# A LayerNorm, linear-attention and expert kernel on eight cores: weight conversions queued first, three input buffers, the phi maps in sequence

## The reference

```python
def phi(x): return elu(x) + 1.0
# attention, for every batch row
q = phi(x @ W_q); k = phi(x @ W_k); v = x @ W_v        # H = 64
for t in range(T):                                     # T = 4096, D = 1024
    S = S + outer(k[t], v[t]); z = z + k[t]
    o[t] = (S @ q[t]) / max(sum(z * q[t]), 1e-6)
attn = o @ W_o
# experts
scores = softmax(x @ gate_w.T); top 2 of 16
y = (1, 0, ..., 0)
for e in range(16):
    out = lmlp(x, W1[e], W3[e], W2[e])                 # silu(x W1) * (x W3), W2
    y = where(hit[e], lresnet(y, out, w[e]), y)        # z / sqrt(z0^2 - |z|^2)
ffn = lresnet(y, lmlp(x, Ws1, Ws3, Ws2), 1.0)
# the layer
x = x + layernorm(attn(layernorm(x)))
x = x + layernorm(ffn(layernorm(x)))
```

## Time and profile before

| what | us |
|---|---|
| median of 2 timed runs | 7395.49 (7387.69 to 7403.29) |
| the profiled execution | 7242.95 |
| its span on the slowest core (core 2) | 7241.3 |
| spans of the 8 cores | 7227.3 to 7241.3 |

### The profile page before, as it was taken

How to read it: one execution, slowest core, us unless ns; L and a number is a source line. 1 busy time by engine, 2 the same in 40 slices (tenths; PEclk the granted TensorE clock), 3 DMA queues, 4 the chain that set the end, 5 groups by cost and what they waited for, 6 DMA issues and landing times.

```text
span 7241.3 us, 86010 instructions; the slowest of 8 cores (7227.3 to 7241.3 us)
## 1 busy us (share of the span) xinstructions
PE 4561.7 (63%) x27764; PEld 2806.4 (39%) x27904; DVE 3662.7 (51%) x8672; ACT 3455.1 (48%) x6173; POOL 42.2 (1%) x39
## 2 busy tenths in 40 slices
PE   3112322257778777787776735787777887777671
PEld 2111222244445444454444523455444554445350
DVE  3112444445555555555555344555555555555434
ACT  2111222236655555555555344555656555565434
POOL 0000000000000000000000000000000000000000
PEclk6555555578888888888787867888878888888786
DMA  4998111121111111211111012111111111111102
GB/s 72 120 121 114 44 58 58 58 88 43 57 58 54 46 43 48 65 54 46 43 46 60 21 64 91 65 55 52 43 43 65 55 52 43 43 65 33 57 15 90
DMA packets 355250, 424.53 MB, mean 59 GB/s; under 512 B 46306, under 2 KB 325602, under 8 KB 348658
## 3 DMA queue, kind: packets, MB, share of 16 engines
q1 hardware_dynamic: 349714, 357.44, 15.7%
q0 software_dynamic: 5088, 61.58, 7.5%
HBM read 438.62 MB, written 103.00 MB: 75 GB/s over the span
## 4 chain that ended last, share of the span: by engine, by line
ACT 33%; PE 31%; DVE 17%; issue 9%; another core or an unknown queue 4%; DMA 4%; DVEq 1%; ACTq 1%; SPq 0%; POOL 0%; POOLq 0%
ACT s_sqs L1016 9%; ACT s_sqs L1041 8%; ACT s_y L1074 8%; PE psA L883 5%; PE psB L883 5%; PE psB L894 5%; PE psA L894 5%; PE p_s1C L883 2%; DMA s_x<-x2sp 2%; DVE s_c L335 2%; PE p_gate L737 2%; DVE s_c L1064 2%; ACT s_c L1055 2%; PE p_s3C L894 2%
## 5 line engine op out<-in xcount | busy, mean ns | idle before, releaser
L988 PE MATMUL psB<-s_we,s_sf 128*128 128x511 bf16 (+1 forms) x1984 | 663.6, 493 | 325.0 <-DVE s_w L1029 319.9
L988 PE MATMUL psA<-s_we,s_sf 128*128 128x511 bf16 (+1 forms) x1984 | 663.8, 493 | 310.3 <-DVE s_w L1029 276.8
L1074 ACT ACTIVATE s_y<-s_w,s_c 128x1024 f32<-128x1024 f32 x544 | 624.5, 1148 | 356.2 <-DVE s_c L1064 353.1
L911 ACT ACTIVATE s_a<-s_s1f,s_beb 128x256 bf16<-128x256 f32 x1152 | 490.8, 496 | 526.9 <-DVE s_s1f L905 525.8
L883 PE MATMUL psA<-s_xtb,s_we 128*128 128x256 bf16 x4096 | 535.6, 296 | 225.4 <-DMA s_xtb<-xtsp 168.7
L932 ACT ACTIVATE s_sq<-s_sf 128x1024 bf16<-128x1024 bf16 (+1 forms) x272 | 301.1, 1107 | 762.7 <-DVE s_sf L927 745.6
L894 PE MATMUL psA<-s_xtb,s_we 128*128 128x256 bf16 x4096 | 536.0, 296 | 173.7 <-DVE s_w L1029 173.7
L1016 ACT ACTIVATE s_sqs<-s_b 128x1023 bf16<-128x1023 bf16 x544 | 575.3, 1058 | 94.8 <-DVE s_b L1013 93.6
L1041 ACT ACTIVATE s_sqs<-s_w 128x1023 bf16<-128x1023 f32 x544 | 566.8, 1042 | 0.5
L883 PEld LDWEIGHTS psA<-s_xtb,s_we 128*128 128x128 bf16 x4096 | 424.3, 106 | 344.3 <-issue 267.8
L894 PEld LDWEIGHTS psA<-s_xtb,s_we 128*128 128x128 bf16 x4096 | 433.0, 106 | 260.6 <-issue 181.2
(11 more groups left out here) (169 smaller groups left out, 6323.1 us busy)
## 6 DMA issues: line engine op xcount, KB each, us to landing
s_xtb<-xtsp SPq DMA_DIRECT2D x272, 512.0 KB, 3.9
s_we<-wec SPq DMA_DIRECT2D x32, 3326.8 KB, 12.9
wec<-wexp POOLq DMA_DIRECT2D x16, 3326.8 KB, 276.3
s_x<-x SPq DMA_DIRECT2D x64, 512.0 KB, 4.1
x2sp<-s_x SPq DMA_DIRECT2D x32, 512.0 KB, 2.6
s_x<-x2sp SPq DMA_DIRECT2D x32, 512.0 KB, 4.3
out<-s_x SPq DMA_DIRECT2D x32, 512.0 KB, 2.9
s_we<-wshc SPq DMA_DIRECT2D x2, 6397.8 KB, 22.1
```

Source lines behind the costliest of these rows:

```text
L911: s.activation(out=s_a[:, it * GRP:(it + 1) * GRP], in_=s_s1f[:, (it - it0) * GRP:(it - it0 + 1) * GRP], func=AF.Silu, bias=bsl[:, it:it + ...
L988: wnh=wnh, pob=pob: t.matmul(pob(nh * 512, nh * 512 + wnh), s_sf[:, sfo + kt * GRP + tt * 128: sfo + kt * GRP + tt * 128 + 128], wsl[:, w2 ...
L1074: s.activation(out=ysl, in_=zsl, func=AF.Identity, scale=rcol),
```

## The change

Three things are changed, all ahead of A3.

1. The 17 converting DMAs are put at the head of the program, behind three memsets on POOL and ahead of POOL's loads of wq, wk, wv and wo, and wait for nothing. The call behind tile 6 is gone.
2. `s_x` has three parts instead of two in A1, with a channel for each, so that three loads can be in flight; the LayerNorm's scalars follow with `cb = 8 * px`. To make room, the attention's constants are put on the stack that is closed behind A3. A3 and the end of the program still use two parts.
3. The three phi maps of a tile are made one behind the other, each by the helper `phi`, all in the same 3 * 128 columns of `s_ph`; each begins behind the addition of the one before. v's two copies stand behind them. The next tile's products in `p_qkv` wait for the last copy alone, which stands last on DVE. In `a2_chunk` the product for the denominator goes into the first columns of `s_ph`.

```diff
+    chXn = chX + [kb.chan("chX2")]
...
-    s_x = es.enter_context(st("s_x", [128, 2 * D], F32))
+    s_x = es.enter_context(st("s_x", [128, 3 * D], F32))
...
-    def emit_weight_conversions(after=()):
+    def emit_weight_conversions():
         tok = None
         for e in range(NE):
             tok = kb.op("G", lambda gp, e=e: gp.dma_start(
-                out=d_wec[e, :, :], in_=d_wexp[e, :, :]),
-                after=after if e == 0 else (), inc=chCv[0], k=16)
+                out=d_wec[e, :, :], in_=d_wexp[e, :, :]), inc=chCv[0], k=16)
         tok = kb.op("G", lambda gp: gp.dma_start(out=d_wshc, in_=d_wsh),
                     inc=chCv[0], k=16)
         return (tok,)
 
-    tok_wcache = None
-
+    tok_wcache = emit_weight_conversions()
...
-    def phi(src_ap, dst_ap, w, after, np_=128, base=0):
+    def phi(src_ap, dst_ap, w, after, np_=128):
         ta = kb.op("V", lambda v: v.tensor_scalar(
-            out=s_ph[0:np_, base:base + w], in0=src_ap, scalar1=0.0,
-            scalar2=None, op0=ALU.min), after=after, inc=chV)
+            out=s_ph[0:np_, 0:w], in0=src_ap, scalar1=0.0, scalar2=None,
+            op0=ALU.min), after=after, inc=chV)
         tb = kb.op("S", lambda s: s.activation(
-            out=s_ph[0:np_, base + w:base + 2 * w],
-            in_=s_ph[0:np_, base:base + w], func=AF.Exp),
+            out=s_ph[0:np_, 128:128 + w], in_=s_ph[0:np_, 0:w], func=AF.Exp),
             after=(ta,), inc=chS)
         tc = kb.op("V", lambda v: v.tensor_scalar(
-            out=s_ph[0:np_, base + 2 * w:base + 3 * w], in0=src_ap,
-            scalar1=0.0, scalar2=None, op0=ALU.max), after=after, inc=chV)
+            out=s_ph[0:np_, 256:256 + w], in0=src_ap, scalar1=0.0,
+            scalar2=None, op0=ALU.max), after=after, inc=chV)
         td = kb.op("V", lambda v: v.tensor_tensor(
-            out=dst_ap, in0=s_ph[0:np_, base + w:base + 2 * w],
-            in1=s_ph[0:np_, base + 2 * w:base + 3 * w],
+            out=dst_ap, in0=s_ph[0:np_, 128:128 + w],
+            in1=s_ph[0:np_, 256:256 + w],
             op=ALU.add), after=(tb, tc), inc=chV)
         return td
...
         p = i % 2
-        cb = 32 * p
-        xsl = s_x[:, p * D:(p + 1) * D]
+        px = i % 3
+        cb = 8 * px
+        xsl = s_x[:, px * D:(px + 1) * D]
         tx = kb.op("Y", lambda y, i=i, xsl=xsl: y.dma_start(
             out=xsl, in_=d_x[i * 128:(i + 1) * 128, :]),
-            after=(g_x[p],) + (tuple(t_consts) if i < 2 else ()),
-            inc=chX[p], k=16)
+            after=(g_x[px],) + (tuple(t_consts) if i < 2 else ()),
+            inc=chXn[px], k=16)
         rstd, mb, tln = ln_stats(xsl, cb, "expln", (tx,))
...
-        g_x[p] = tln1
+        g_x[px] = tln1
...
-                af = (tfm,) + g_qkv if (fi == 0 and k == 0) else ()
+                af = (tfm, g_qkv) if (fi == 0 and k == 0) else ()
...
         g_lnf[p] = tmm
+        tok_qf[i] = phi(p_qkv[0:64, 0:128], s_qf[0:64, i * 128:(i + 1) * 128],
+                        128, (tmm,), np_=64)
+        tok_qt[i] = phi(p_qkv[:, 256:320], s_qt[:, i * H:(i + 1) * H],
+                        64, (tok_qf[i],))
+        tok_kt[i] = phi(p_qkv[:, 320:384], s_kt[:, i * H:(i + 1) * H],
+                        64, (tok_qt[i],))
         tok_vf[i] = kb.op("V", lambda v, i=i: v.tensor_copy(
             out=s_vf[0:64, i * 128:(i + 1) * 128], in_=p_qkv[0:64, 128:256]),
             after=(tmm,), inc=chV)
         tok_vt[i] = kb.op("V", lambda v, i=i: v.tensor_copy(
             out=s_vt[:, i * H:(i + 1) * H], in_=p_qkv[:, 384:448]),
             after=(tmm,), inc=chV)
-        specs = [
-            (p_qkv[0:64, 0:128], s_qf[0:64, i * 128:(i + 1) * 128], 128, 64, 0),
-            (p_qkv[:, 256:320], s_qt[:, i * H:(i + 1) * H], 64, 128, 384),
-            (p_qkv[:, 320:384], s_kt[:, i * H:(i + 1) * H], 64, 128, 576),
-        ]
-        tas, tcs, tbs, tds = [], [], [], []
-        for src, _, w, np_, base in specs:
-            tas.append(kb.op("V", lambda v, src=src, w=w, np_=np_, base=base:
-                             v.tensor_scalar(
-                out=s_ph[0:np_, base:base + w], in0=src, scalar1=0.0,
-                scalar2=None, op0=ALU.min), after=(tmm,), inc=chV))
-            tcs.append(kb.op("V", lambda v, src=src, w=w, np_=np_, base=base:
-                             v.tensor_scalar(
-                out=s_ph[0:np_, base + 2 * w:base + 3 * w], in0=src,
-                scalar1=0.0, scalar2=None, op0=ALU.max), after=(tmm,),
-                inc=chV))
-        for j, (_, _, w, np_, base) in enumerate(specs):
-            tbs.append(kb.op("S", lambda s, w=w, np_=np_, base=base:
-                             s.activation(
-                out=s_ph[0:np_, base + w:base + 2 * w],
-                in_=s_ph[0:np_, base:base + w], func=AF.Exp),
-                after=(tas[j],), inc=chS))
-        for j, (_, dst, w, np_, base) in enumerate(specs):
-            tds.append(kb.op("V", lambda v, dst=dst, w=w, np_=np_, base=base:
-                             v.tensor_tensor(
-                out=dst, in0=s_ph[0:np_, base + w:base + 2 * w],
-                in1=s_ph[0:np_, base + 2 * w:base + 3 * w],
-                op=ALU.add), after=(tbs[j], tcs[j]), inc=chV))
-        tok_qf[i], tok_qt[i], tok_kt[i] = tds
-        g_qkv = (tok_vf[i], tok_vt[i], tok_qf[i], tok_qt[i], tok_kt[i])
+        g_qkv = tok_vt[i]
...
-        if i == 7:
-            tok_wcache = emit_weight_conversions(after=(tok_vt[6],))
```

More of the change, by code:

```diff
@@ L245, in build_nc @@
     s_sqs = es.enter_context(st("s_sqs", [128, D], BF16))
[L246 to L255, removed]
     s_wte = es.enter_context(st("s_wte", [128, NT * 16], F32))
@@ L281, in emit_weight_conversions @@
         return (tok,)
-    tok_wcache = None
+    tok_wcache = emit_weight_conversions()
+    esA = contextlib.ExitStack()
+    pt = nc.psum_tensor
+    s_wqb = esA.enter_context(st("s_wqb", [128, 8 * H], BF16))
+    s_wkb = esA.enter_context(st("s_wkb", [128, 8 * H], BF16))
+    s_wvb = esA.enter_context(st("s_wvb", [128, 8 * H], BF16))
+    s_wob = esA.enter_context(st("s_wob", [H, D], BF16))
+    s_gw = esA.enter_context(st("s_gw", [128, 8 * 16], F32))
+    s_idf = esA.enter_context(st("s_idf", [128, 128], F32))
+    s_idb = esA.enter_context(st("s_idb", [128, 128], BF16))
+    s_utf = esA.enter_context(st("s_utf", [128, 128], F32))
+    s_utb = esA.enter_context(st("s_utb", [128, 128], BF16))
+    s_onesb = esA.enter_context(st("s_onesb", [1, 128], BF16))
     def ld(dst, src):
@@ L306, in build_nc @@
         return nc
-    esA = contextlib.ExitStack()
-    pt = nc.psum_tensor
     s_qf = esA.enter_context(st("s_qf", [128, T], BF16))
@@ L317, in build_nc @@
     s_lnf = esA.enter_context(st("s_lnf", [128, 2 * D], BF16))
-    s_ph = esA.enter_context(st("s_ph", [128, 832], F32))
+    s_ph = esA.enter_context(st("s_ph", [128, 3 * 128], F32))
     s_S = esA.enter_context(st("s_S", [64, 2 * H], F32))
@@ L396, in build_nc @@
     p_of = esA1.enter_context(pt("p_of", [64, 128], BF16))
-    g_x = [None, None]
+    g_x = [None, None, None]
     g_trA = None
-    g_qkv = ()
+    g_qkv = None
     tok_qf = [None] * NT
@@ L544, in a2_chunk @@
         td1 = kb.op("V", lambda v, c=c: v.tensor_tensor(
-            out=s_ph[:, 768:832], in0=p_zc[:, :],
-            in1=s_qt[:, c * H:(c + 1) * H],
+            out=s_ph[:, 0:H], in0=p_zc[:, :], in1=s_qt[:, c * H:(c + 1) * H],
             op=ALU.mult), after=(tz2, tok_qt[c]), inc=chV)
@@ L549, in a2_chunk @@
         td2 = kb.op("V", lambda v, cb=cbase: v.tensor_reduce(
-            out=C(cb), in_=s_ph[:, 768:832], axis=AX.X, op=ALU.add),
+            out=C(cb), in_=s_ph[:, 0:H], axis=AX.X, op=ALU.add),
             after=(td1,), inc=chV)
```

## The result

The changed kernel is slower: the ratio of its time to that of the kernel before is **1.0483, 95% interval 1.0435 to 1.0531**. Over all runs the medians are 7638.11 us (11 runs, 7571.99 to 7778.98) and 7395.49 us (10 runs, 7238.12 to 7441.02; the first two alone happen to have the same median); in part of the runs of either kernel a die had a lower clock, which the ratio leaves out, so the quotient of these medians is smaller than the ratio. The new profiled execution took 7577.08 us, against 7242.95: +334, where +321 was forecast.

A forecast was written before the change was run, and what follows sets the result against it. The prediction took DMA, with the software queue worked off in order, to bound A1: later start +555, phi maps +54, A1's regained time -288, so +321 us on the median 7395.5, giving 7717 us, range 7545 to 7775.

The forecast's parts named there:

- What bounds, and who waits: DMA bounds A1 from 116 to 710 us; moved ahead, the conversions make wo, x and all of A1 wait; chance 0.88.
- How long the conversions take alone: Conversions at the head, without x's loads beside them: 0.94 of 593.7 us, 558 us, with ends of 523 and 594.
- four readings: Conversions' time without x, as share of 593.7 us: unchanged, memory traffic 0.96, engines' time 0.93, bytes as written 0.88.
- Start of A1: First use of x, behind the conversions and wo: 570 us instead of 14.3, +555 us.
- What A1 gets back: A1 without conversions beside it runs at its free pace of 15.58 us a tile and regains 288 us.
- The phi maps: Three maps in sequence in each A1 tile: 3.54 against 1.87 us, 1.7 us a tile, +54 us; bounds 0 to 83.
- The third buffer: Third load of x in flight in A1: costed at nothing, as with free engines x comes in time with two.
- The sum: Whole kernel: 555 + 54 - 288 = +321 us, 7564 us profiled, 7717 us when added to the median of 7395.5.
- the likeliest case's own range: Whole kernel, software queue worked off in order: +280 to +360 us, 7675 to 7755 us; chance 0.88.
- full stretch: A1 from 116 to 710 us, DMA share 0.99 at 120 GB/s; taken as 19.3 tiles in 594 us.
- The rival that used the average: wo overtakes the conversions, A1 starts near 15 us, tile 31 ends at 825: +41 us, 7437 us; overtaking chance 0.07.
- its best version: Overtaking, with a third load giving x half as much again: A1 ends at 661, -123 us, 7272 us; chance 0.01.

The follow-up runs named there:

- run with the weights first: Changed kernel with the conversions still at the head but behind POOL's loads of wq, wk, wv and wo; tile 31 at 845.41 us, experts start at 1588.37 us.
- cut pieces: The 16 expert conversions each cut into 7 column pieces of 1901 values; span 7092.9 us on the kernel before, 7730.2 us on the changed kernel.
- the run of part 2: Kernel before with only the third buffer for x added; experts start at 1508.83 us, moved by -16.5 us.
- part 1 alone: Kernel before with only the 17 conversions moved to the head of POOL, ahead of wq to wo; span 7530.2 us, experts start moved by +271.5 us.

## Why the prediction was right

- **What bounds, and who waits.** Right: wo landed behind all conversions, with x and A1 behind it. The run with the weights first shows that it is the place in the queue, as it changes nothing else. One reading of the row was loose: slices 2 to 4 of the earlier trace rows are 9, 9 and 8, not "9 or 1"; the table by stage, on which the argument rests, was read rightly.
- **How long the conversions take alone.** I took 0.94 of 593.7, 558 us; they took 571.4 - 1.6 = 569.8, a factor of 0.960. Of the four readings the one by traffic with memory, 0.957, came out, and the one by the engines' time (0.93) was off: with x gone, 10.98 MB went in 100 us with 99.8% of the engines' time, so a packet took longer to serve. By the rows the traffic is 3 x 10.98 = 32.9 MB in 100 us, 33.1 with x before. With cut pieces it is 31.0 alone and 31.2 with x: again the same sum with x and without, at another level. The Trainium skill (DMA: Bandwidth & Descriptors, Specifications) has a limit of some 358 GB/s for a core's traffic with memory; 329 to 331 is 8% below it. No run here moved that limit, and the sum depends on the packets, so that it is what binds isn't shown.
- **Start of A1.** +563.5 against +555 (577.8 against 14.3): the conversions took 12 us more, and the steps ahead of them and behind them some 4 less.
- **What A1 gets back.** -288 held: 17.24 a tile without a wait for x. 563.5 + 31 x 1.66 - 288 = 327, and tile 31 moved by 326.8.
- **The phi maps.** 1.7 us a tile and 54 in all against 1.66 and 53.
- **The third buffer.** Nothing is left for it in the changed kernel's sum, as forecast. By itself, in the kernel before, it is worth 16.5 us.
- **What follows.** The experts were to be the same: 5716 and 5722 us.
- **The sum.** +321 against +334: the start of A1 was 8 too low, and the expert stage had 5.5 more. On the profiled execution's own time I had 7564 and it took 7577. The predicted 7717 lies above the median of 7638 since I added the 321 to a median that stood 152 us above the profiled execution; the changed kernel's stands only 61 above its own. So 7638 lies below the likeliest case's own range, 7675 to 7755, and inside the full one by the room left at its low end for just that. The sum of parts is borne out part by part; where in the range the median fell is luck.
- **Where the reading was wrong without harm.** I took the full stretch as 19.3 tiles at one pace. It was 14 intervals of about 37 us and then the free pace, as the last conversion has small packets. The sum used only its total, 288. The rival that used the average was priced 20 us too low (825 against 845 in the run that made it real). And its best version, in which a third load brings half as much again, fell with the run of part 2.

## What to carry to other kernels

A load that the first instruction needs must not stand behind bulk transfers in the same queue: that alone was 266 us here, for four loads of 128 KB. Where bulk must run beside loads that are waited for, look at bytes in a packet, not at the DMA share or the loads in flight: cut to the size of the others' packets it cost A1 nothing. And move bulk only to where its pieces fit a measured slack; beside A3 and beside the experts, which looked idle by their DMA share of 0.17 to 0.19, each us of full engines cost 0.5 to 0.8 us, until the bulk came in pieces of 0.5 MB, one a tile.

## What the runs showed of the hardware

- The engines served the software and the hardware queue one packet for one with two loads of x waiting (395 to 395) and with three (397 to 395). With cut pieces in A1 it was 2761 to 867, which stays open, and in A3 7644 to 6579. The Trainium skill (DMA: Bandwidth & Descriptors, Queues, rings and completion order) states such turns by packet between queues, and the trace agrees where the packets are large. What wasn't expected is how far the packets differ for the same program line's kind of copy: 27 KB for the form 112x15208, 2.6 KB for 2512x1304, 3.4 KB on average for pieces of 128x1901.
- Small packets cost the conversions 6% alone (10.34 against 10.98 MB in 100 us), and POOL stood still 476 us before it could issue the DMA behind 112 of them, where 17 large ones went out in 10 us. What POOL has to do soon must stand ahead of such a row.
- TensorE's granted clock didn't set A1's pace. In the changed kernel it was 1.00 from 594 to 760 us (the upper level, 2.4 GHz), 0.76 from 760 to 930 and 0.51 from 930 to 1111 (nearly all at the lower level, 1.2 GHz), and a tile took 17.2 to 17.3 us in all three. That PE had stood still for 574 us doesn't explain the high start: with part 1 alone it had stood still as long, and the clock was 0.57 from 590 to 750 us.
